# A fused attention and feed-forward block: the row maxima of the next head are transposed at the fifth place of a step instead of the sixth, and copied behind the fourth exponential instead of the fifth

## The reference

```
scores = einsum('bhqd,bhkd->bhqk', Q, K) / sqrt(32)     # Q, K after the rotation
scores = where(causal, scores, -inf)
attn   = softmax(scores, axis=-1)                       # 32 (batch, head) pairs, 1024 x 1024 each
out    = einsum('bhqk,bhkd->bhqd', attn, V)
```

## Time and profile before

| what | value |
|---|---|
| median of 3 runs | 758.27 us |
| the runs | 757.69, 758.27, 768.73 us |
| profiled execution, its own time | 768.15 us |
| its span | 766.4 us |
| TensorE busy in the span | 743.2 us (97%) |
| VectorE, ScalarE, GpSimd busy | 438.5, 307.4, 247.0 us |
| mean granted TensorE clock | 0.988 |
| share of TensorE in the chain that ended last | 84% |
| share of the DMA of the maxima in that chain | 3% |

### The profile page before, as it was taken

One profiled execution on the slowest core, in us unless ns is written; L12 is line 12 of the kernel. 1 busy time (PEld: TensorE's weight loads), 2 busy tenths in 40 slices (PEclk: granted clock), 3 DMA queues, 4 the chain that ended last, 5 costly groups with the idle time before them and its releaser, 6 DMA issues.

```text
span 766.4 us, 10665 instructions
## 1 busy us (share of the span) xinstructions
PE 743.2 (97%) x3563; PEld 539.6 (70%) x3563; DVE 438.5 (57%) x1103; ACT 307.4 (40%) x641; POOL 247.0 (32%) x224
## 2 busy tenths in 40 slices
PE   7999999989999999999999999999999999999996
PEld 7888888755555556566546547787788888888884
DVE  7978765895775767677767726773324114214112
ACT  3323132265664656566646564222332222223221
POOL 0815153311113141414231426932223223224223
PEclk9999999989999999999999999999999999999998
DMA  8677468643665666667656556670001001001001
GB/s 279 228 268 261 172 259 269 248 140 101 170 170 144 166 163 169 171 166 183 170 143 166 139 161 159 231 321 1 0 1 56 0 1 55 0 0 56 0 1 57
DMA packets 54318, 104.39 MB, mean 136 GB/s; under 512 B 14820, under 2 KB 18404, under 8 KB 53748
## 3 DMA queue, kind: packets, MB, share of 16 engines
q1 hardware_dynamic: 54264, 103.72, 44.3%
HBM read 69.62 MB, written 38.21 MB: 141 GB/s over the span
## 4 chain that ended last, share of the span: by engine, by line
PE 84%; DMA 4%; issue 4%; DVE 2%; POOL 2%; ACT 2%; SPq 1%; DVEq 0%; POOLq 0%; ACTq 0%
PE ps L1101 37%; PE ps L1240 17%; PE ps L1126 9%; PE ps L1316 9%; PE ps L1219 9%; DMA q_st<-neg_max_T 3%; PE ps L1093 2%; POOL hid_lo L592 1%; PE ps L1160 1%; ACT o_raw L687 1%; ACT p L680 1%; DMA l_cols<-o_raw 1%; SPq L421 0%; PE ps L1137 0%; DMA rec_l<-rec_rows 0%
## 5 line engine op out<-in xcount | busy, mean ns | idle before, releaser
L680 ACT ACTIVATE p<-ps 128x384 f32<-128x384 f32 (+3 forms) x384 | 160.7, 487 | 74.8 <-PE ps L1219 74.2
L841 DVE CUSTOM_DVE_ANT_0 masked<-ps,mask_qk 128x512 bf16<-128x512 f32 (+1 forms) x240 | 114.4, 503 | 80.3 <-PE ps L1126 79.0
L1219 PE MATMUL ps<-q_st,k_st 99*128 99x384 f32 (+2 forms) x384 | 136.4, 373 | 6.0 <-DMA q_st<-neg_max_T 4.9
L1240 PE MATMUL ps<-p,v_slot 128*64 128x512 f32 (+3 forms) x768 | 141.6, 506 | 0.2 <-ACT o_raw L687 0.2
L1126 PE MATMUL ps<-k_st,q_st 96*128 96x512 f32 (+2 forms) x384 | 132.3, 366 | 2.0 <-DVE row_max L841 1.7
L1052 DVE SCALAR_TENSOR_TENSOR hid<-ps,us_sb,silu 128x512 f32<-128x512 f32 x44 | 33.0, 751 | 165.3 <-PE ps L1101 159.6
L592 POOL TENSOR_TENSOR hid_lo<-hid,hid_hi 128x512 fp32r<-128x512 f32 x44 | 56.7, 1289 | 172.4 <-ACT hid_hi L756 172.4
L561 POOL TENSOR_SCALAR_AFFINE_SELECT p<-p 128x512 f32<-128x512 f32 x64 | 40.8, 642 | 215.4 <-ACT p L680 215.4
L1240 PEld LDWEIGHTS ps<-p,v_slot 128*64 128x64 f32 x768 | 51.3, 140 | 78.0 <-issue 65.4
L1126 PEld LDWEIGHTS ps<-k_st,q_st 96*128 96x128 f32 x384 | 72.7, 190 | 32.4 <-issue 21.8
L1219 PEld LDWEIGHTS ps<-q_st,k_st 99*128 99x128 f32 x384 | 72.9, 191 | 25.3 <-ACT p L680 8.9
(11 more groups left out here) (119 smaller groups left out, 1074.2 us busy)
## 6 DMA issues: line engine op xcount, KB each, us to landing
qk_scratch<-st_hi SPq DMA_DIRECT2D x32, 512.0 KB, 3.8
q_st<-qk_scratch SPq DMA_DIRECT2D x32, 384.0 KB, 4.4
k_st<-qk_scratch SPq DMA_DIRECT2D x32, 384.0 KB, 5.1
flag_st<-in_ffn SPq DMA_DIRECT2D x32, 264.0 KB, 2.8
ffn_copy<-in_ffn SPq DMA_DIRECT2D x32, 264.0 KB, 3.4
qk_scratch<-st_lo SPq DMA_DIRECT2D x16, 512.0 KB, 3.9
o_T<-o_raw SPq DMA_DIRECT2D x32, 128.0 KB, 4.8
rec_l<-rec_rows SPq DMA_DIRECT2D x32, 128.0 KB, 3.3
```

Of the source, the lines that this page charges most:

```text
L680: act.activation(p32[:, at:at + q0 + w - keep], ps[:, ST_BANK + i % ST_RING, keep - q0:w], ACT.Exp, scale=SCALE).then_inc(exp_done, 1)
L841: ins = dve.tensor_tensor_reduce((masked_a if u < 2 else masked)[:, s_before(i) % 2, col:col + kept], scores, mask_qk[:, 512 - kept:512], ...
L1219: pe.matmul(ps[:, ST_BANK + i % ST_RING, 0:w], k_st[0:K_ALL, slot, kt * P:(kt + 1) * P], q_st[0:K_ALL, slot, q0:q0 + w], start=True, stop= ...
L1240: ins = pe.matmul(ps[VW * a:VW * (a + 1), o_bank(u, half), q0 - 512 * half:512], v_slot[:, slot, kt, :], p32[:, at:at + n], start=(kt == 0 ...
```

## The change

Two constants change. `M_ENTRY` goes from 5 to 4: the transposition now has the fifth place, directly behind the first group of products, and the fifth score piece (128 x 512, query tile 3) moves from place 4 to place 5. `M_AFTER` goes from 4 to 3: ScalarE copies the transposed maxima behind the exponential of piece 3, and so, in even steps, ahead of the evacuation of the first half. By the formulas in the code, `M_BANK` goes from bank 1 to bank 0, the score piece that moved from bank 0 to bank 1, the transposition waits for the reduction of place 0 instead of place 1, and the place that waits for the copy is 8 instead of 9. The early list of heads 0 and 1 in stage A takes the same order. No operation is added or removed.

```diff
-M_ENTRY = 5
-M_AFTER = 4
+M_ENTRY = 4
+M_AFTER = 3
 S_BANKS = [[piece] for piece in S_PIECES[:-2]] + [S_PIECES[-2:]]
 S_BANKS.insert(M_ENTRY, [])
```

## The result

The changed kernel is faster by 0.8%. Over 20 runs each, its median is 754.3 us (751.84 to 759.39) against 760.76 (756.98 to 768.73); the ratio is 0.9921, with a 95% interval of 0.9899 to 0.9943, which is 6.0 us. I had forecast 758.9, no change, within 753 to 766. The median of before over 20 runs is 2.5 us above that of the three runs that I had.

A forecast was written before the change was run, and what follows sets the result against it. TensorE, busy nearly throughout, was taken to bound the kernel. Without stalls, 3.8 - 3.5 + 0.3 = +0.6 on 758.27 gives 758.9 us, no change (with stalls, 768.15 + 0.6 - 9 = 759.7); own range 756 to 761.5, wider 753 to 766.

The forecast's parts named there:

- What bounds, and the two parts of the sum: TensorE bounds; the sum is what every step pays plus what stalls for the maxima give back, where an execution has them.
- Odd steps, -0.25 each: 14 odd steps: copy moves into ScalarE's idle time, fifth and sixth exponentials start sooner; -3.5 us, bounds 0 and 0.35 each.
- Even steps, +0.25 each: 15 even steps: copy and evacuation precede the fifth exponential, shifted piece 7 comes 0.39 late, part comes back; +3.8 us.
- the evacuation for 0.60: ScalarE, even steps: the evacuation holds the next operation for 0.60 us, so the fifth exponential starts at 311.45.
- Steps 0 and 1, +0.3: No products cover VectorE; the transposition still waits for L859, the score piece now runs behind it: +0.3 us for both.
- The waits in an execution that has them, -9: TensorE's five stalls for the maxima, with the slow clock behind: 9 of 10.2 us go if they land 0.7 sooner.
- the doubtful one: DMA of the maxima: copy leaves about 0.7 us sooner and landing follows; doubted, since ring order would land nothing earlier.
- The median has no such waits: Unprofiled runs: 768.15 without 10.2 us is 757.9, near runs of 757.69 and 758.27, so the median run holds no stalls.
- no stalls: The kernel before, in an execution without waits for the maxima: 757.9 us, from the profiled 768.15 without 10.2.
- The odd steps: Faster rival, chance 0.22: even steps lose 0.1, odd ones gain 0.35, -3.1 us in all, so 755.2 us.
- a slow start that moves to the transposition: Faster rival's reason, even steps: the transposition takes over the slow start behind the products, so they lose only 0.1.
- The slower one: Rival on ScalarE's order, chance 0.16: even steps lose 0.45 each waiting for the transposition, odd gain nothing; 765.4 us.

The follow-up runs named there:

- e5: Kernel before, with SP issuing the maxima ahead of the finished outputs only in steps 0, 4, 8, ...; ratio 0.9955, median 755.96 us.
- e6: Changed kernel, with SP issuing the maxima ahead of the finished outputs only in steps 0, 4, 8, ...; ratio to before 0.9912.
- e1: Kernel before with only the transposition moved (M_ENTRY 5 to 4), M_AFTER staying 4; ratio to before 0.9944.
- e9: Changed kernel, SP holding the maxima's transfers until shifted piece 6 in steps 4, 8, 12, ..., where they are late; ratio to before 0.9934, median 754.50 us.
- e10: Changed kernel, SP holding the maxima's transfers until shifted piece 6 in steps 3, 7, 11, ..., one before the late ones; ratio to before 0.9969, median 758.32 us.
- e2: Kernel before with only the copy moved (M_AFTER 4 to 3), M_ENTRY staying 5; ratio to before 1.0097.
- e4: Kernel before, with SP issuing the maxima ahead of the finished outputs in all even steps that move outputs; ratio to before 1.0045.
- e3: Changed kernel with the evacuation ahead of the copy in even steps; ratio to before 0.989.
- e7: Changed kernel, evacuation ahead of the copy in even steps, and SP issuing maxima ahead of finished outputs in steps 0, 4, 8, ...; ratio to before 0.9869, median 749.98 us.
- e8: Kernel before with the copy one exponential later (M_AFTER 4 to 5), transposition unmoved; ratio to before 1.0076.

## Why the prediction was wrong

The measured 754.3 lies in the range, and the change is clear of its noise in a direction that I had not forecast. Point by point:

- *What bounds, and the two parts of the sum.* Right: steps and waits are separate, and e5 and e6 show them apart in the traces.
- *Odd steps, -0.25 each.* Measured -0.31, near my upper bound. The copy went into ScalarE's idle time, and both waits for the sixth and fifth exponential shrank.
- *Even steps, +0.25 each.* Measured +0.08. The step of the prediction that failed is "the evacuation for 0.60". I read the distance between two starts, 310.46 and 311.06, as what the first costs the second. It was the wait for shifted piece 4: started at 310.68 and done 0.34 later, at 311.02. The changed kernel and e1 have 0.48 for the same two operations. The copy also came 0.32 us behind the transposition, not 0.36. Piece 7 was 1.49 us behind the start of the place instead of 1.28, late by 0.21 instead of 0.39, and 0.13 of it came back. So of a loss of 0.25 only 0.08 was there.
- *Steps 0 and 1, +0.3.* About right. The transpositions there wait 1.14 us each for L859, where they waited 0.71 and 0.56, and from the first shifted piece of step 0 to that of step 2 it is 12.82 us in e6 against 12.43 in e5, so +0.4.
- *Steps together.* I had +3.8 - 3.5 + 0.3 = +0.6 us. Measured: 15 x 0.08 - 14 x 0.31 = -3.1 us, and -2.7 with the 0.4 of steps 0 and 1. The pair of undisturbed steps says the same: 18.32 - 18.55 = -0.23, about 15 times.
- *The waits in an execution that has them, -9.* Measured 10.2 to 2.1, so -8.1. The size was right; the way was the doubtful one. I gave 0.7 us of each wait to the earlier issue. e9 shows that as worth nothing, and e10 that what is ahead in the queue is worth over half; it moved up by 0.38 us (3.64 to 4.02), where I had guessed 0.4. So the size came out close in part by luck: most of it was counted for a cause that is worth nothing.
- *The median has no such waits.* This failed too and cost as much as the even steps (2.7 us and 2.6 us). I took 10.2 from 768.15 and found 757.9, beside 757.69 and 758.27. But the profiled execution held one more disturbance that I had left in: TensorE's clock at 0.5 for 6.8 us from 168.2, in step 1, which took 11.92 us there and 8.14 in e5. e5, with neither, was profiled at 753.8 us, 4 below my "no stalls". The match was a coincidence of two numbers.
- *The sum as measured.* Steps -2.7, with steps 0 and 1; waits, in runs without profile, -3.4 (e5 against before) and 0.7 of it still left (e6 against after), so -2.7; together -5.4, where the times give -6.0. The intervals of these ratios are 2 us wide on either side, so the terms of the waits are not known as closely as the sum suggests.
- *The rivals.* The odd steps won, with 22% of my chances, and with the rival's own -3.1 us. Its reason for the cheap even step, a slow start that moves to the transposition, is not what the rows show: 0.12 of the 0.17 that I had too much is the evacuation's price. The slower one is real but needs the transposition where it was (e2). Of "faster, same, slower by 2%" the forecast of same was right, but the 20 runs tell far less than 2% from no change: their interval is 0.2% to either side.

The window from 165 to 176 us, of before and of after, shows the disturbance that I had missed, in the granted clock (third from the end). TensorE had waited for VectorE four times in the 10 us before it, for 0.44 to 0.71 us each. It is gone in the trace after:

```profile
165.00:176.00 11.00, 9.96 (x38) 5.60 (x37) 7.12 (x25) 5.00 (x12) 1.61 (x3) 0.69 0.52 150
```

```profile
165.00:176.00 11.00, 9.87 (x53) 6.66 (x52) 10.46 (x39) 7.86 (x20) 2.60 (x5) 1.00 0.78 235
```

## What to carry to other kernels

The distance between two starts on one engine is the cost of the first only if the second was ready; look up what it waits for before using it as a price, above all in a stretch where two engines take turns. When a transfer lands late, look at what was issued before it on the same queue, one step back: here moving that was worth more than issuing the late one sooner, and moving the rest behind it was best, as long as nobody is waiting for the rest (e4 against e5). And don't call a run undisturbed because one subtraction makes it fit: count all the stretches of slow clock first.

## What the runs showed of the hardware

- TensorE's clock is a part of the scatter. In the changed kernel's trace it was at 1.2 GHz for 3.4 us during the first weights' products; TensorE was busy in that stretch, but had just waited 1.95 us for VectorE. The profiled runs of e2, e4, e6 and e9 have the same, wait and slow clock. Those of before, e1, e3, e5, e7, e8 and e10 have waits of 1.11 to 1.70 us at that place and no slow clock. The first transposition is at about 153 us with it and at 150 to 151 without. So spans of single profiled runs can't be compared to better than 3 us here; stretches can. Among the runs of the kernel before beside e5 to e8, the fastest (756.74 us) has a mean clock of 0.998 and the slowest (768.62) one of 0.990, by which I estimate that the clock is about half of the distance between them.

```profile
9.93:13.34 3.41, 3.41 (x17) 3.41 (x18) 3.41 (x5) 2.63 (x5) 0.00 (x0) 0.50 0.69 195
```

- The length of a wait alone did not say whether the clock would fall. In stage B, waits of 1.58 and 1.09 us (before) and of 0.96 us (e1) were followed by 3.4 us at 1.2 GHz; waits of 1.34 (e4), 1.11 (e3) and 1.09 us (e10) were not. So one profiled run can hold or lack several us of excess that way.
- The lengths of undisturbed steps repeat to about 0.02 us within a run and between runs with the same order on the compute engines (to 0.04 in e3), where whole executions scatter by 7 us and more.
- An evacuation of 128 x 512 that lasts 0.57 to 0.59 us lets the next operation of ScalarE start after 0.48, so its duration is more than what it costs the one behind it.
